# Exact float32r parts in both feed-forwards of an eight-layer hybrid network on one core

## What is computed

```python
h = jnp.einsum('bsd,dh->bsh', x, W_exp) + b_exp
h = butterfly(h, up_weights, D_HIDDEN)
h = jax.nn.gelu(h + up_bias, approximate=False)
h = butterfly(h, down_weights, D_HIDDEN)
y = jnp.einsum('bsh,hd->bsd', h, W_con) + b_con
return y + down_bias
```

## Time and profile before

| what | value |
|---|---|
| median of 3 runs | 2668.12 us (2667.52 to 2676.39) |
| profiled execution | 2671.26 us, its span 2669.2 us |
| TensorE busy in the span | 2289.9 us |
| VectorE, ScalarE, GpSimd busy | 1659.8, 1372.6, 1200.8 us |
| first feed-forward, by TensorE's matmuls | 663 to 908 us of the span |
| second feed-forward, the same | 1666 to 1891 us |

### The profile page before, as it was taken

One profiled execution on the slowest core, in us unless ns is written; L12 is line 12 of the kernel. 1 busy time (PEld: TensorE's weight loads), 2 busy tenths in 40 slices (PEclk: granted clock), 3 DMA queues, 4 the chain that ended last, 5 costly groups with the idle time before them and its releaser, 6 DMA issues. The chain is left out here.

```text
span 2669.2 us, 55063 instructions
## 1 busy us (share of the span) xinstructions
PE 2289.9 (86%) x20336; PEld 1601.9 (60%) x20336; DVE 1659.8 (62%) x4170; ACT 1372.6 (51%) x2116; POOL 1200.8 (45%) x1245
## 2 busy tenths in 40 slices
PE   7957777777999888988889987889899879999979
PEld 4535555555666555555555554778566756666658
DVE  6757778776113477767767764666444447777753
ACT  4522222222332288877887885442311457777653
POOL 4329999991001177656756752122365003223220
PEclk9979999998999899999999999999999989999999
DMA  5554445541000111111111111000000100000001
GB/s 179 151 173 135 141 142 153 160 136 63 17 1 28 40 57 56 63 52 57 49 56 53 59 51 42 8 1 1 1 0 1 38 0 1 1 1 1 1 1 64
DMA packets 158733, 149.00 MB, mean 56 GB/s; under 512 B 21441, under 2 KB 141377, under 8 KB 155393
## 3 DMA queue, kind: packets, MB, share of 16 engines
q1 hardware_dynamic: 138704, 105.51, 13.2%
q0 software_dynamic: 3456, 23.07, 2.5%
q10 hardware_dynamic: 16304, 16.83, 2.1%
HBM read 100.51 MB, written 40.63 MB: 53 GB/s over the span
## 5 line engine op out<-in xcount | busy, mean ns | idle before, releaser
L1838 POOL TENSOR_SCALAR a_dist<-a_dist,a_mq 128x512 f32<-128x512 f32 x512 | 357.1, 719 | 120.9 <-ACT a_mq L1777 120.9
L1881 DVE TENSOR_SCALAR_CACHE_REDUCE a_dist<-a_ring 128x512 f32<-128x512 f32 x512 | 332.1, 687 | 90.0 <-PE a_ring L1526 88.6
L1767 ACT ACTIVATE a_pT<-a_psT 128x1024 f32<-128x1024 f32 x256 | 258.3, 1025 | 95.4 <-PE a_psT L1538 87.7
L1538 PE MATMUL a_psT<-ident,a_dist 128*128 128x128 f32 x2048 | 266.3, 277 | 18.0 <-ACT a_pT L1767 17.8
L1538 PEld LDWEIGHTS a_psT<-ident,a_dist 128*128 128x128 f32 x2048 | 235.0, 142 | 50.2 <-issue 20.4
L1761 ACT ACTIVATE a_dist<-a_dist 128x2048 f32<-128x2048 f32 x128 | 236.9, 1902 | 45.1 <-DVE a_dist L1881 42.1
L1526 PE MATMUL a_ring<-a_stack 102*128 102x512 bf16 x512 | 184.2, 398 | 59.1 <-DVE a_dist L1881 35.1
L1526 PEld LDWEIGHTS a_ring<-a_stack 102*128 102x128 bf16 x512 | 47.6, 98 | 230.1 <-DVE a_dist L1881 165.3
L3359 ACT ACTIVATE ds_wtm<-ds_wg,ds_par 128x256 f32<-128x256 f32 x64 | 29.1, 502 | 268.2 <-DVE ds_wg L3489 264.0
L1551 PE MATMUL a_psO<-a_pT,a_va 128*32 128x512 f32 x1024 | 138.0, 616 | 2.3 <-ACT a_pT L1767 2.3
L517 POOL CAST f_h_hi<-f_h 128x512 fp32r<-128x512 f32 x64 | 46.4, 727 | 202.8 <-ACT f_h L506 202.8
(11 more groups left out here) (432 smaller groups left out, 5845.2 us busy)
## 6 DMA issues: line engine op xcount, KB each, us to landing
a_stack<-a_parts_dram SPq DMA_DIRECT2D x384, 64.0 KB
a_parts_dram<-a_parts SPq DMA_DIRECT2D x32, 384.0 KB, 2.5
bf_w<-in_up_w_dram POOLq DMA_DIRECT2D x10, 1024.0 KB
bf_w<-in_down_w_dram POOLq DMA_DIRECT2D x10, 1024.0 KB
ds_nbg<-tok_nbk ACTq DMA_DIRECT2D x128, 64.0 KB
feat_v<-di_part SPq DMA_DIRECT2D x16, 256.0 KB, 2.6
tok_nbk<-di_nbk SPq DMA_DIRECT2D x16, 256.0 KB, 3.0
feat_k<-di_part SPq DMA_DIRECT2D x16, 256.0 KB, 3.4
```

Source lines behind the costliest of these rows:

```text
L1538: last = turn(psT[:, u % 2, kb, q * P:(q + 1) * P], dist[:, g % 2, i, q, k * P:(k + 1) * P], core.ident[:])
L1767: a(pT[:, u // 2, u % 2], psT[:, u % 2], ACT.Exp).then_inc(exp_done, 1)
L1838: last = nc.gpsimd.tensor_scalar(d, d, -1.0, mq[:, g % 2, i, q:q + 1], ALU.mult, ALU.add)
L1881: ts(dist[:, gg % 2, i, q, :], ps[:], 1e-12, 3.0e38, ALU.max, ALU.min, accum_out=mq[:, gg % 2, i, q:q + 1]).then_inc(ring_out, 1)
```

## The change

- One class `FeedForward` is left, the former `SplitFeedForward`, and both stages use it. The first stage's products thus become three float32r products of parts. Its tiles lie at written-out places in the attention's memory: the weight parts where `pT` lies, the gelu's parts in `dist[:, 0]`, x's parts and the gelu's rows in `dist[:, 1]`. Its second transpose bank stays shared with psY (`shared`), with the two waits that go with it.
- The gelu's rows have four buffers in place of two (`RING`).
- The cast of the gelu's rows goes from GpSimd to VectorE, right ahead of the subtraction (`parts_of_hidden`).
- The next batch's four normalisations stand one each behind gelus 1 to 4.
- In the second stage the wide tap steps go from VectorE to GpSimd (`gpsimd`, 25 steps), except two rounding steps. VectorE keeps the small ones, at other places: ahead of tile 0 and of the row additions of batch 1, ahead of the row additions of batch 3, ahead of tile 0 of batch 4. ScalarE's two larger parts come one batch later.
- In the first stage VectorE's attention pieces are spread over the tiles of batches 5 to 7.
- `inv`, `w` and `b` of the convolution are loaded at the start of `conv_spectra`, no longer at the start of the second feed-forward; the waits follow.

The core of the diff (the former class `FeedForward` is deleted in full and not shown):

```diff
-class SplitFeedForward:
...
+    RING = 4
+    def __init__(self, nc, core, bf, tag, tile, h_lo, psT, psH, psY, back=()):
+        self.nc, self.core, self.bf, self.back = nc, core, bf, back
+        self.shared = len(psT) == 1
+        self.psT, self.psH, self.psY = psT + psY[1:] if self.shared else psT, psH, psY
...
+        self.up_hi = tile("up_hi", [P, KD, HID], F32R)
...
+        self.h = tile("h", [P, self.RING, S], F32)
...
+                if self.shared and b >= 2 and k == 1:
+                    pe.wait_ge(self.x_done, TPB * (b - 1))
...
+            if self.shared and j == 1 and b + 1 < B:
+                pe.wait_ge(self.x_lo_done, KD * (b + 2))
...
+        def normalize(b, j):
+            if b and j == 0:
                 act.wait_ge(self.tr_done, KD * b)
-            for j in range(TPB):
-                t = TPB * b + j
-                nc.scalar.activation(self.xn[:, j, :], core.X[:, t, :], ACT.Identity, bias=core.shift[:, t:t + 1],
-                                     scale=core.rstd[:, t:t + 1]).then_inc(self.xn_done, 1)
...
-                if n >= 2:
-                    act.wait_ge(self.h_lo_done, n - 1)
-                nc.scalar.activation(self.h[:, m % 2, :], psH[m % 2], ACT.Gelu,
+                if n >= self.RING:
+                    act.wait_ge(self.h_lo_done, n - self.RING + 1)
+                nc.scalar.activation(self.h[:, n % self.RING, :], psH[m % 2], ACT.Gelu,
                                      bias=self.bf.bias_h[:, m:m + 1]).then_inc(self.h_done, 1)
-                if m == NH // 2 and b + 1 < B:
-                    normalize(b + 1)
+                if b + 1 < B and m in (1, 2, 3, 4):
+                    normalize(b + 1, m - 1)
             if b + 1 < B:
                 take_turned(b + 1)
...
-    def gpsimd(self, pool):
-        for n in range(B * self.NH):
-            pool.wait_ge(self.h_done, n + 1)
-            self.nc.gpsimd.tensor_copy(self.h_hi[:, n % self.NH, :], self.h[:, n % 2, :]).then_inc(self.h_hi_done, 1)
...
-        def rest_of_hidden(b, m):
-            dve.wait_ge(self.h_hi_done, NH * b + m + 1)
-            tt(self.h_lo[:, m, :], self.h[:, m % 2, :], self.h_hi[:, m, :], ALU.subtract).then_inc(self.h_lo_done, 1)
+        def parts_of_hidden(b, m):
+            n = NH * b + m
+            dve.wait_ge(self.h_done, n + 1)
+            nc.vector.tensor_copy(self.h_hi[:, m, :], self.h[:, n % self.RING, :]).then_inc(self.h_hi_done, 1)
+            dve.wait_ge(self.h_hi_done, n + 1)
+            tt(self.h_lo[:, m, :], self.h[:, n % self.RING, :], self.h_hi[:, m, :],
+               ALU.subtract).then_inc(self.h_lo_done, 1)
...
-                rest_of_hidden(b, m)
-                if m == NH // 2 - 1:
-                    between(b, 0)
+                between(b, m)
+                parts_of_hidden(b, m)
             if b + 1 < B:
                 rest_of_turned(b + 1)
-            between(b, 1)
+            between(b, NH)
             for j in range(TPB):
...
-            ffn.gpsimd(pool)
+            beside.gpsimd(nc, pool)
...
+    def load_forward(self, sp):
+        sp.dma_start(self.fwd[:], self.sources[0].rearrange("(k p) n -> p k n", p=P)).then_inc(self.fwd_in, 16)
...
-            pe.wait_ge(self.vec, self.TAPS)
+            pe.wait_ge(self.wide, self.TAPS)
...
-        if n == 2:
-            act.wait_ge(self.vec, self.PHASES)
+        if n == 3:
+            act.wait_ge(self.vec, self.WHOLE)
+            act.wait_ge(self.wide, self.PHASES)
...
+        if (n, m) == (1, FeedForward.NH):
+            dve.wait_ge(self.wide, self.RAW)
...
+        if (n, m) == (3, FeedForward.NH):
...
+        if (n, m) == (4, 0):
...
+    def gpsimd(self, nc, pool):
...
+        pool.wait_ge(self.loaded, 48)
+        pool.wait_ge(self.vec, self.STEPS)
+        step(tt(f3[0], over_i(TURN), ix, ALU.mult))
+        step(tt(g_im[:], over_j(TURN), jx, ALU.mult))
+        step(tt(self.g_mag, over_j(DR), jx, ALU.mult))
+        pool.wait_ge(self.vec, self.WHOLE)
+        step(tt(f[:, 0, :], f[:, 0, :], f[:, 1, :], ALU.subtract))
+        step(tt(f3[1], over_i(DR), ix, ALU.mult))
+        step(tt(g_im[:], g_im[:], g_re[:], ALU.subtract))
+        pool.wait_ge(self.act_n, self.ROOTS)
+        step(tt(f[:, 2, :], f[:, 2, :], f[:, 1, :], ALU.mult))
+        step(tt(f[:, 3, :], f[:, 3, :], f[:, 1, :], ALU.mult))
+        pool.wait_ge(self.act_n, self.POWERS)
+        step(tt(g_im[:], g_im[:], self.g_mag, ALU.mult))
+        step(tt(g_re[:], g_re[:], self.g_mag, ALU.mult))
+        pool.wait_ge(self.vec, self.MODES)
+        step(tt(f3[0], over_i(NRE), f3[3], ALU.mult))
+        step(tt(f3[1], over_i(NIM), f3[2], ALU.mult))
+        step(tt(self.f_re[:], f3[0], f3[1], ALU.subtract))
+        step(tt(f3[0], over_i(NRE), f3[2], ALU.mult))
+        step(tt(f3[1], over_i(NIM), f3[3], ALU.mult))
+        step(tt(self.f_im[:], f3[0], f3[1], ALU.add))
+        step(ts(self.f_im[:], self.f_im[:], -1.0, None, ALU.mult))
+        for q in range(2):
+            for c in range(CPT):
                 dst = self.fm[:, q].rearrange("p t (i c) -> p t i c", c=CPT)[:, :, :, c]
                 step(ts(dst, (self.f_re, self.f_im)[q][:], self.chan[:, c:c + 1], None, ALU.mult))
...
-            pe.wait_ge(lc.loaded, 64)
+            pe.wait_ge(lc.fwd_in, 16)
...
+                if i == 0 and u == 0:
+                    pe.wait_ge(lc.loaded, 48)
...
+        word, half = 4, HPT * TPB * S * 4
+        at_rows = at_dist + half + (2 * KD * S + TPB * D) * word
+        places = {"up_hi": at_weights, "up_lo": at_weights + KD * HID * word, "down": at_weights + 2 * KD * HID * word,
+                  "h_hi": at_dist, "h_lo": at_dist + half // 2, "xn": at_rows, "x_hi": at_rows + TPB * D * word,
+                  "x_lo": at_rows + (TPB * D + KD * S) * word, "h": at_rows + (TPB * D + 2 * KD * S) * word}
+        tile = lambda n, shape, dtype: nc.alloc_sbuf_tensor_at(f"f1_{n}", shape, dtype, offset=places[n])
+        ffn = FeedForward(nc, core, bf, "f1", tile, places["h_lo"], [psO[:]], [psT[:, 0, n, :] for n in range(2)],
+                          [psT[:, 1, n, :] for n in range(2)])
...
+            def first_batch(b, m):
+                if (b, m) == (4, 0):
                     scale(0, TPB, 1)
-                if b == 5:
+                if (b, m) == (5, 0):
                     dve.wait_ge(loaded, 144)
                     ts(nbq[:], bqk[:, 0], -2.0, None, ALU.mult).then_inc(nbq_done, 1)
                     dve.wait_ge(nbq_done, 1)
+                if (b, m) == (5, 2):
                     for k in range(KD):
                         take_rows(None, k)
-                if b in (5, 6):
-                    take_projection(None, zero, 2 * b - 10)
-                    take_projection(None, zero, 2 * b - 9)
-                if b == 6:
+                if (b, m) in ((5, 5), (5, 7), (6, 3), (6, 6)):
+                    take_projection(None, zero, ((5, 5), (5, 7), (6, 3), (6, 6)).index((b, m)))
+                if (b, m) == (6, FeedForward.NH):
                     first_length(None, zero)
                     other_lengths(None, zero)
-                if b == 7:
+                if (b, m) == (7, 3):
                     dve.wait_ge(va_set, 2)
-                    for j in range(TPB):
-                        take_v(None, zero, j)
+                if b == 7 and m in (3, 5):
+                    take_v(None, zero, m - 3)
+                    take_v(None, zero, m - 2)
             ffn.vector(dve, first_batch)
```

More of the change, by code:

```diff
@@ L280 @@
     NH = HID // P
[L282 to L301, removed]
-                for j in range(TPB):
[L303 to L317, removed]
-                for k in range(KD):
-                    last = nc.tensor.matmul(psH[m % 2], bf.up[:, k, m * P:(m + 1) * P], xnT[:, b % 2, k, :],
-                                            start=(k == 0), stop=(k == KD - 1))
-                last.then_inc(self.h_ps, 1)
-                between(b, m)
-            if b + 1 < B:
-                turn(b + 1)
-            pe.wait_ge(self.h_done, NH * (b + 1))
-            for j in range(TPB):
-                if TPB * b + j >= 2:
-                    pe.wait_ge(self.x_done, TPB * b + j - 1)
-                if j == 1 and b + 1 < B:
-                    pe.wait_ge(self.xnT_done, KD * (b + 2))
-                for m in range(NH):
-                    last = nc.tensor.matmul(psY[j % 2][:, 0:D], h[:, b % 2, m, j * P:(j + 1) * P],
-                                            bf.down[:, m, :], start=(m == 0), stop=(m == NH - 1))
-                last.then_inc(self.y_ps, 1)
@@ L496, in take_turned @@
                 nc.scalar.activation(self.x_hi[:, k, :], psT[k], ACT.Identity).then_inc(self.x_hi_done, 1)
-        normalize(0)
+        for j in range(TPB):
+            normalize(0, j)
         take_turned(0)
@@ L557, in add_rows @@
             nc.vector.bn_stats(core.bn[:, t, :], core.X[:, t, :]).then_inc(self.bn_done, 1)
-        dve.wait_ge(bf.back[0], 16)
+        for loaded in self.back[0:1]:
```

(12 more changed lines are left out.)

178 lines of the change are left out of this document (55 added, 123 removed).

## The result

| | before | after |
|---|---|---|
| median | 2671.80 us (2667.52 to 2676.39, 4 runs) | 2641.49 us (2636.16 to 2652.24, 4 runs) |
| ratio | | 0.9879, 95% interval 0.9844 to 0.9914 |
| profiled execution, its span | 2671.26, 2669.2 us | 2636.16, 2634.2 us |

The account below looks back on a forecast made before the run. First stage bounded by TensorE's arithmetic, second by VectorE's order. 45.1 - 1.0 - 3.5 - 7 = 33.6 saved, less 10 lost, is 23.6; from 2671.3 that makes 2647.7, at the median 2644 us, range 2604 to 2662.

Parts of the forecast that it names:

- The arithmetic of the first stage: First feed-forward, TensorE: float32r batches take 23.1 us against 28.74, saving 5.64 per batch and 45.1 in eight.
- Its VectorE work: First feed-forward: splitting gelu tiles on VectorE stays hidden by 0.5 us; attention's projections and lengths in batches 5 and 6 cost 7.
- The start: Start of first feed-forward: splitting up weights costs 1.0 us, casts waiting for GpSimd's stack clearing 3.5, bounds 0 and 7.
- The second stage: Second feed-forward: 235 us after against 225.6 before, so 10 lost, because GpSimd's tap steps hold VectorE's casts and subtractions.
- batch 1 was to lose 10: Second feed-forward: three GpSimd products among sixteen VectorE part operations lose 9 us, two rounding steps ahead of row additions 1.
- Batch 4 was to lose 25: Second feed-forward: VectorE 6.5 us late, then six products and nine one-input GpSimd steps alternate with its sixteen operations: 25 us lost.
- The turn-taking: Second feed-forward: VectorE gets one cast or two-SBUF-input operation per GpSimd step; sources from PSUM are not delayed.
- rival C: Slower than before: GpSimd's last eight strided steps in batch 4 take 6 us each or more; at 7.5, 2693 us; chance 0.05.
- The loads: Three convolution loads moved to the spectra block cost 0, their first reader standing tens of microseconds behind.
- A: GpSimd and VectorE overlap after all: second stage 197 us, a gain of 28, total 2606; chance 0.24.
- B: Same mechanism, dearer: clearing holds the cast (3.5 more), projections cost 12, GpSimd's steps 15% slower: 2660 us; chance 0.13.
- D: VectorE casts at one element per cycle, 1.3 us per tile; first stage keeps its gain less 2 us; inside the forecast.

Follow-up runs that it names:

- the thinned run: Changed kernel with all 25 of GpSimd's tap steps on one column, taps not computed: second stage 195.5 us against 223.5, ratio 0.9806 to the kernel before.
- the two runs with thinned steps: Changed kernel with all 25 GpSimd tap steps cut to one column, or only the first 17: second stage 195.5 and 202.4 us, ratios 0.9806 and 0.9855.

## Why the prediction was right, step by step

**The arithmetic of the first stage.** Predicted 23.1 us a batch and 45.1 in eight; measured 23.42 and 42.6 (8 x 5.32). The figure came from the second stage, where 23.1 holds; in the first the gelu tiles come 1.40 us apart, in the second 1.36. Why, no run here shows.

**Its VectorE work.** Hidden by 0.5 in undisturbed batches: right, TensorE's timeline has no wait in batches 1 to 4, and a tile's parts take VectorE the 1.06 us that I had put. Batches 5 and 6 together were priced at 7 us over TensorE's own pieces, bounds 2 and 14. Before, they had 66.1 us, 8.6 over two bare batches of 28.74; after 66.8, 19.9 over two of 23.42. So 11.3 was lost, inside the bounds. Batch 7 takes some of it back: over all three it is 98.2 before and 91.0 after, and 8.8 lost. The largest single piece is one that I had not priced: the wait for the squares, 3.81 us, and behind it 4 us (837.88 to 842.00) with a granted clock of 0.61.

**The start.** The split's 1.0 is exact (1.03). The clearing was put at 3.5, half of an interval of 0 to 7, because no row showed a cast beside one. It was 7.75, just over the upper bound, since both clearings hold a cast and not only the long one (1.83 and 5.93 us). A middle between "not held" and "held" is a value that could not come; naming the two cases would have been better. The first stage in all gave 25.7 (34.45 - 8.78) where 33.6 had been forecast. The 1.93 us that after is ahead at the first transpose are no part of it: that stretch varies by over 15 us between profiles with the same code there.

**The second stage.** Predicted 235, measured 223.5. By its own items: batch 1 was to lose 10, and lost 7.3 over both of its distances (31.7 + 21.8 - 46.2). Batch 3 was to lose 5; its distance has 3.9 too much, of which 2.1 only move into the next one, as the thinned run shows. Batch 4 was to lose 25 and lost 20.8 (38.8 + 28.2 - 46.2), or 22.9 with these 2.1. The 2 for a lower clock and the 1 for the others didn't show separately. The turn-taking, the step on which this rested, is shown by the rows, by the two runs with thinned steps and by the one with the steps on VectorE. What failed is its extension to all of GpSimd's steps. I counted nine one-input steps of 1.4 in strict turn. They take 2.86 and 3.97 us, 2 and 2.8 times as much, and hold VectorE for part of that (1.9 of each 4.1 us). Two errors with opposite signs, and that they nearly cancel is luck; the sum came out 4 high. Had the strided steps been in strict turn, as I assumed, *and* as long as they are, rival C's way would have been open: up to eight turns of 4 us in batches 4 and 5. That is argued, not measured.

**The loads.** Put at 0. No wait on them shows. After the second stage the two profiles differ by 1.3 us (777.8 and 776.5), but that is not shown to be theirs: with the loads moved this stretch took 776.3 to 780.5 us, with the loads as before 777.8 and 778.0.

**The rivals.** A is refuted: GpSimd's steps cost the stage 28 us, where A had them cost nothing. Its 197 us for a stage without them is near the 195.5 measured. Of B's three parts the clearing held, and batches 5 and 6 lost 11.3 where it had put 12 for the projections; but GpSimd's products are not 15% slower (2.00 to 2.69 us in batch 4 against 2.36). C's length of step came true in part (3.97 us of the 6 needed), but not its turn. D did not come: a cast of 512 columns takes 0.43.

Two misses, 7.9 us too much gain in the first stage and 11.5 too little in the second, partly cancel: the two stages gained 27.8 where 23.6 had been forecast. The median gained 30.3. The 2644 comes closer still, to 2.5 us, because the median before that it was taken from, 2668.12, moved to 2671.80 with a fourth run. So the mechanism was right, and the closeness of the total is in good part luck.

## What to carry to other kernels

Work moved to GpSimd is not beside VectorE's work if VectorE has casts or subtractions of SBUF tiles there: 25 steps that cost VectorE 35 us took 28 us from the stage on GpSimd and 5 to 7 us where VectorE did them itself in its gaps. Read what stands *beside* the moved instructions, in both stages, and count turns, not busy time. And where an unknown has two discrete outcomes, keep them as two cases instead of forecasting their mean.

## What the hardware showed

- A GpSimd clearing holds a VectorE cast to its end (2.52 and 6.62 us in place of 0.69), but not a bias addition or a subtraction of two SBUF tiles (0.41, 1.22). The rule of the Trainium skill that I had drawn on (GPSIMD Engine Reference, § 1. Specifications) names VectorE instructions in a two-port mode and those with two SBUF inputs; for those with two SBUF inputs it holds beside GpSimd's products, but not beside a clearing.
- A GpSimd product of two inputs holds one such operation of either kind for its whole length, also where it writes every fourth float (2.25 us beside steps of 2.21). A one-input step holds less: 1.9 of 4.1 us where it writes every fourth float, 0.9 of 3.0 where it writes whole rows (1.48 in place of 0.69 for the subtraction, 0.53 in place of 0.43 for the cast). A subtraction from PSUM is not held: 0.68 us beside such steps too, and all 32 row additions of the stage took 0.42 to 0.43.
- On GpSimd 1024 columns took 2.0 to 2.7 us as a product of two inputs, 2.86 times a constant, 2.97 times a scalar operand, 3.97 with every fourth float written, and 2.21 in that last form with the scalar broadcast as a second input. The attention's one-input step takes 0.73 for 512; what makes it so much cheaper, no run here tells. The Trainium skill (GPSIMD Engine Reference, § 2.1 Instruction dispatch) puts two inputs at about 2.5 cycles per element for the one read port they share; with the 1.2 GHz of its § 1 that is an estimate of 2.1 us, and the rows agree nearly (2.00 is the shortest). By the same reason one input should be the faster form; the rows say otherwise.
